# Masking the spread column norms on GpSimd, and scaling and masking in one VectorE operation

## What is computed

```python
# layer 0, per batch; h = relu(layernorm(x)), adj is a 0/1 matrix of 128 x 128
z_l, z_g, v = h @ W_lang.T, h @ W_grav.T, h @ W_V.T
zn  = z_l / max(norm(z_l), 1e-8)
A_l = max(zn @ zn.T, 0) * (1 - eye)                  # language similarities
d2  = max(sq + sq.T - 2 * z_g @ z_g.T, 0)
A_g = exp(-d2 / (2 * sigma**2)) * (1 - eye)
K   = w_l * row_stochastic(A_l * adj) + (1 - w_l) * row_stochastic(A_g * adj)
x   = x + (K @ v) @ W_O.T
# layer 1; h2 = relu(layernorm(x))
x   = x + adj.T-weighted sum of h2 over the nodes + bias
```

## Time and profile before

| what | value |
|---|---|
| time, median of 3 runs | 1271.28 us (1269.57 to 1271.44) |
| the profiled execution, its own time | 1269.61 us |
| its span in the trace | 1267.7 us |
| TensorE busy, share of the span | 1241.2 us, 98% |
| VectorE | 1058.5 us, 83% |
| ScalarE | 694.5 us, 55% |
| GpSimd | 574.7 us, 45% |
| granted TensorE clock, mean | 0.996 |

### The profile page before, as it was taken

One profiled execution on the slowest core, in us unless ns is written; L12 is line 12 of the kernel. 1 busy time (PEld: TensorE's weight loads), 2 busy tenths in 40 slices (PEclk: granted clock), 3 DMA queues, 4 the chain that ended last, 5 costly groups with the idle time before them and its releaser, 6 DMA issues.

```text
span 1267.7 us, 22572 instructions
## 1 busy us (share of the span) xinstructions
PE 1241.2 (98%) x6324; PEld 1039.6 (82%) x6324; DVE 1058.5 (83%) x1826; ACT 694.5 (55%) x1324; POOL 574.7 (45%) x964
## 2 busy tenths in 40 slices
PE   7999999999999999999999999999999999999996
PEld 6878888888888888888888888888888888888884
DVE  5678888988888988888898888898888898888777
ACT  5346555456645456655446655546655545654543
POOL 1115553434554434554434555444555443455433
PEclk9999999999999999999999999999999999999998
DMA  6232424342333343333343232344242444243201
GB/s 243 34 72 81 106 54 95 99 108 81 102 71 78 99 108 87 95 79 70 99 108 97 86 93 56 99 108 103 79 108 49 99 101 108 79 103 69 47 34 66
DMA packets 308894, 112.55 MB, mean 89 GB/s; under 512 B 269840, under 2 KB 269968, under 8 KB 308880
## 3 DMA queue, kind: packets, MB, share of 16 engines
q1 hardware_dynamic: 177360, 95.78, 27.2%
q10 hardware_dynamic: 131520, 16.60, 7.9%
HBM read 46.20 MB, written 33.62 MB: 63 GB/s over the span
## 4 chain that ended last, share of the span: by engine, by line
PE 93%; DVE 4%; ACT 1%; issue 1%; DMA 1%; POOL 0%; SPq 0%; DVEq 0%; ACTq 0%
PE ring L866 75%; PE p_ps L866 15%; PE p_ps L939 2%; PE kt_ps L879 1%; DMA h2f<-in_L_gnn_W_grav 1%; DVE x_out L688 0%; DVE bn L568 0%; DVE y_lo L557 0%; ACT h L379 0%; DVE bn L637 0%; DVE x_ring L631 0%; DVE y_lo L784 0%; DVE deg L602 0%; DVE v_lo L784 0%; DVE hT_lo L557 0%
## 5 line engine op out<-in xcount | busy, mean ns | idle before, releaser
L301 POOL TENSOR_TENSOR x_out<-x_ring,bias_sb 128x512 f32<-128x512 f32 x128 | 162.8, 1295 | 499.9 <-DVE bn L637 499.9
L866 PE MATMUL ring<-hT_hi,Lw_hi 128*128 128x512 f32 x640 | 256.9, 401 | 4.9 <-DVE hT_lo L576 2.1
L406 ACT ACTIVATE y_hi<-ring 128x512 fp32r<-128x512 f32 x256 | 148.3, 592 | 206.5 <-PE ring L866 203.7
L866 PE MATMUL ring<-hT_hi,Lw_lo 128*128 128x512 f32 x640 | 250.6, 392 | 0.0
L866 PE MATMUL ring<-hT_lo,Lw_hi 128*128 128x512 f32 x640 | 250.2, 391 | 0.0
L866 PE MATMUL ring<-MT_hi,hT_hi 128*128 128x512 f32 x512 | 203.0, 396 | 0.0
L557 DVE TENSOR_TENSOR v_lo<-ring,v_hi 128x512 fp32r<-128x512 f32 x128 | 88.5, 692 | 136.8 <-ACT v_hi L442 136.8
L866 PE MATMUL ring<-MT_hi,hT_lo 128*128 128x512 f32 x512 | 200.0, 391 | 0.0
L866 PE MATMUL ring<-MT_lo,hT_hi 128*128 128x512 f32 x512 | 199.9, 390 | 0.0
L308 POOL TENSOR_TENSOR h_lo<-h2f,h_hi 128x512 fp32r<-128x512 f32 x124 | 158.0, 1296 | 84.8 <-ACT h_hi L476 84.8
L557 DVE TENSOR_TENSOR y_lo<-ring,y_hi 128x512 fp32r<-128x512 f32 x256 | 169.2, 680 | 28.4 <-ACT y_hi L406 28.3
(11 more groups left out here) (160 smaller groups left out, 2537.0 us busy)
## 6 DMA issues: line engine op xcount, KB each, us to landing
x_ring<-in_x SPq DMA_DIRECT2D x32, 1024.0 KB, 5.5
out<-x_out SPq DMA_DIRECT2D x128, 256.0 KB, 2.2
h_turned<-h SPq DMA_DIRECT2D x248, 64.0 KB, 2.1
h_turned<-h ACTq DMA_DIRECT2D x248, 64.0 KB, 2.1
rn_cols<-rn_dram SPq DMA_DIRECT2D x31, 256.0 KB, 3.9
x_ring<-in_L_gnn_W_lang SPq DMA_DIRECT2D x4, 256.0 KB, 5.6
h2f<-in_L_gnn_W_grav SPq DMA_DIRECT2D x1, 1024.0 KB, 9.2
chain<-in_L_gnn_W_O SPq DMA_DIRECT2D x1, 1024.0 KB, 13.0
```

What stands on the lines that cost most here:

```text
L301: pool.tensor_tensor(x_out[:, b], x_rows(g, b), bias_sb[:, :], ALU.add).then_inc(x2b_ready, 1)
L406: act.activation(y[0][:, a, :, l], bank(n).rearrange("p (b m) -> p b m", b=GB), ACT.Copy)\
L866: mm = pe.matmul(out, lhsT, rhs, start=(k == 0), stop=(k == len(terms) - 1))
```

## The change

`rn_dram` and `rn_cols` are laid out batch by batch, with the nodes contiguous; the store to DRAM therefore writes single elements. GpSimd multiplies `rn_cols` in place by the mask (`mask_norms`) behind its four `h2_lo`, and waits for the spread there. VectorE's `similarities` is gone; `mask_l` now takes the maximum of A and 0 and multiplies by the masked `rn_cols` in one operation, and waits for `rn_masked`. Only the last group keeps two operations (`mask_l_last`). `a_ready` counts two steps per group instead of three.

```diff
-        rn_cols = sb("rn_cols", [P, P, GB])
+        rn_cols = sb("rn_cols", [P, GB, P])
-        rn_dram = nc.dram_tensor("rn_dram", [P, GB], F32).ap()
+        rn_dram = nc.dram_tensor("rn_dram", [GB, P], F32).ap()
...
             def spread_norms(g):
                 sp.wait_ge(rn_step, RN_STEPS * g + 1)
-                sp.dma_start(rn_dram, rn[:, 0]).then_inc(rn_stored, 16)
+                sp.dma_start(rn_dram.rearrange("b p -> p b"), rn[:, 0], allow_slow_non_contiguous=True).then_inc(rn_stored, 16)
                 sp.wait_ge(rn_stored, 16 * g + 16)
-                sp.dma_start(rn_cols[:, :, :], rn_dram.unsqueeze(0).to_broadcast([P, P, GB])).then_inc(rn_spread, 16)
+                sp.dma_start(rn_cols[:, :, :], rn_dram.unsqueeze(0).to_broadcast([P, GB, P])).then_inc(rn_spread, 16)
...
+            def mask_norms(g):
+                pool.wait_ge(rn_spread, 16 * g + 16)
+                by_col = mask[:, :].unsqueeze(1).to_broadcast([P, GB, P])
+                pool.tensor_tensor(rn_cols[:, :, :], rn_cols[:, :, :], by_col, ALU.mult).then_inc(rn_masked, 1)
...
                     for b in range(GB):
                         h2_lo(i - 1, b)
+                if after:
+                    mask_norms(i)
...
-            def similarities(g, last=False):
-                if last:
-                    dve.wait_ge(r_done, 1)
-                else:
-                    dve.wait_ge(rn_spread, 16 * g + 16)
-                dve.wait_ge(s_ready, g + 1)
-                by_col = r_ps[:, :, :] if last else rn_cols[:, :, :].rearrange("p m b -> p b m")
-                dve.tensor_tensor(A[:, :, 0], A[:, :, 0], by_col, ALU.mult).then_inc(a_ready, 1)
             def mask_l(g):
-                dve.wait_ge(a_ready, 3 * g + 1)
+                dve.wait_ge(rn_masked, g + 1)
+                dve.wait_ge(s_ready, S_STEPS * (g + 1))
+                dve.scalar_tensor_tensor(out=A[:, :, 0], in0=A[:, :, 0], scalar=0.0,
+                                         in1=rn_cols[:, :, :],
+                                         op0=ALU.max, op1=ALU.mult).then_inc(a_ready, 1)
+
+            def mask_l_last(g):
+                dve.wait_ge(r_done, 1)
+                dve.wait_ge(s_ready, S_STEPS * (g + 1))
+                dve.tensor_tensor(A[:, :, 0], A[:, :, 0], r_ps[:, :, :], ALU.mult).then_inc(a_scaled, 1)
+                dve.wait_ge(a_scaled, 1)
                 dve.scalar_tensor_tensor(out=A[:, :, 0], in0=A[:, :, 0], scalar=0.0, in1=maskb,
                                          op0=ALU.max, op1=ALU.mult).then_inc(a_ready, 1)
```

More of the change, by code:

```diff
@@ L30, in gnn_pair @@
     RN_STEPS = 2
+    S_STEPS = 1
     blk = {ac: n for n, ac in enumerate(TRI)}
@@ L171, in gnn_pair @@
         diag_ready = sem("diag_ready")
-        rn_step = sem("rn_step")
+        rn_step, rn_masked, a_scaled = sem("rn_step"), sem("rn_masked"), sem("a_scaled")
         def passes(hi_lo_lhs, hi_lo_rhs):
@@ L600, in row_factors @@
             def row_factors(g):
-                dve.wait_ge(a_ready, 3 * g + 3)
+                dve.wait_ge(a_ready, 2 * g + 2)
                 dve.tensor_reduce(deg[:, 0], A, AX.X, ALU.add).then_inc(deg_step, 1)
@@ L738, in iteration @@
                         output(i - 1, b, n + b)
-                similarities(i)
                 mask_l(i)
@@ L768, in last_chain @@
                 sum_s(i)
-                similarities(i, last=True)
-                mask_l(i)
+                mask_l_last(i)
                 mask_g(i)
```

## The result

The changed kernel took **1412.55 us** (median of 5 runs, 1411.79 to 1414.38) against 1271.28: ratio 1.1121 (95% interval 1.1106 to 1.1137), 141 us slower. The profiled execution took 1411.79 us, with a span of 1410.0.

What follows compares the result with a forecast made beforehand. TensorE was taken as busy nearly throughout, the turn's end hanging on GpSimd's `h_lo` chain from the eighth y block. Gains of 2.0 and 0.3 us, 2.3 in sum, took 1271.28 to 1269.0 us; range 1261.5 to 1275.

Steps and rivals of the forecast that it cites:

- The store: On SP's queue: 512 runs of 4 bytes take 2.5 us until the spread may go, bounds 1.7 and 5.6.
- rival B: Slow store delays GpSimd's `mask_norms`; TensorE pays one for one beyond a 5.2 us store; 1282 at 5.6; chance 0.12.
- 0.73 us free behind 640.3: From 640.3 on, delaying GpSimd's `mask_norms` costs nothing up to today's `KT_lo`, 0.73 us; beyond that one for one.
- `hT_lo` at about 1 us: On VectorE at the turn's end: `hT_lo` is stretched to about 1 us by GpSimd's `h_lo`.
- GpSimd's operation: `mask_norms`, 128x512, behind the last `h_lo`: taken at 1.28 us, bounds 1.28 and 2.0.
- Rival A: Turn's end hangs on ScalarE's copies, so the whole K·v wait is gained: 9.2 us plus 0.3, 1261.8; chance 0.12.
- the K·v wait: First weight load of the K·v products waits for `kt_split`: 0.33 us of TensorE per turn, to go in 28 turns.
- Rival C: `mask_norms` starts before `hT_lo`, so the first `x_out` comes 1.28 us later: 36 us, 1307; chance 0.05.
- Rival D: Nothing arrives: merged operation dearer (1.07), or small operations excluded long enough to use up the lead: 1271.3; chance 0.16.
- The sum of 2.3 us: Total gain: 28 x 0.07 = 2.0 us, plus 0.3 at the fifth y block's weight load waiting for `y_lo`.
- the third residual addition: On VectorE, it waits for the third K·v product; an earlier K·v gains 0.07 us per turn, 2.0 in 28.
- The place of the new wait: `mask_norms` waits for the spread on GpSimd, before `norm1`; norms usable from about 640.3, spread lands at 638.3, hidden.

Runs made afterwards that it cites:

- the first experiment: Changed kernel with the old store and norms layout (128 runs of 16 bytes, node by node), L592 reading the norms strided: 1265.38 us, ratio 0.9963.
- the fifth: Kernel of the first experiment, with the statistics of the group's last two residual additions ahead of all of the next group's: 1257.55 us, ratio 0.9896.
- the second experiment: Kernel before with only the new store and layout; L586 and L592 stay apart, nothing goes to GpSimd: 1338.52 us, ratio 1.0536.

## Why the prediction was wrong

**The step that failed is "The store".** The prediction bounded the new store by 1.7 us (the old store) and 5.6 (the `scal` loads at the start) and took 2.5, from the row of `h` with as many runs. It took 8.7, in the kernel and by itself. Both neighbours were chosen by the number and size of runs; what counted was how the runs lie against each other in DRAM. The turns of `h` have 512 runs each, and 512 runs that lie apart take only 2.7 us, near what I took; 512 side by side take 8.7. The upper bound was no better: a load says nothing about neighbouring writes, and no row of before showed 4-byte writes side by side. With no neighbour of the same kind the top of the range should have stood open, and with it rival B's share, which I held at 0.12 because the slack of 1.9 us looked ample.
The rule of the Trainium skill cited there (DMA: Bandwidth & Descriptors, Rules for kernel authors), that a strided last dimension becomes one descriptor per element and should be rearranged, pointed the right way. Descriptors alone do not explain the price: 2.7 us against 8.7 for the same 512 elements.

**Rival B was the mechanism, with two terms off.** It said one for one, and the turns show 1.52 against 1.55. It let the cost begin at a store of 5.2 us, with 0.73 us free behind 640.3, which is 0.72 us before the turn's start. Extended to a turn of 37.61, the changed kernel's line has the cost begin 0.75 us before the turn's start, so of the 0.73 nothing is left, and the point is a store of about 9.15 − 0.75 − 3.9 = 4.5 us. The later turn shown above gives the reason. From the end of L307 to `normalize` it takes 681.63 − (675.99 + 1.26) = 4.38 us; the prediction had 607.5 + 37.74 − 641.6 = 3.64, and the 0.74 between them is as much as the margin. `norm1`'s small operations now run while VectorE works through L592 and `y_lo`, and two of them take 0.68 and 0.67 us, where such an operation alone takes 0.20. The prediction had allowed 0 to 0.6 us for that and not set it against the margin. And the spread lands after 4.8 us, not 3.9. Worked by its own line, (8.7 − 5.2 + 0.9) x 28 = 123 us; with the point at 4.5, (8.7 − 4.5 + 0.9) x 28 = 143; measured 141, or 147 over the kernel with the old store.

**What held.** With the store left as it was, the rest came as foreseen: `hT_lo` at about 1 us (0.99), the first weight load 0.6 us behind `x_out` (0.55), a turn of 37.66 (37.65 in the one shown, 37.61 on average), `normalize` 0.89 us later where 0.65 was worked out, and L592 at 0.69 us where it reads contiguously (1.08 with the stride). GpSimd's operation was taken at 1.28: it took 1.27 in the changed kernel, but 1.54 here, where it starts beside `hT_lo`. Rival A falls: the K·v wait is gone in the first experiment and its time did not come, until the fifth moved the chain too. Rival C does not occur: `hT_lo` starts before L307 (637.35 against 637.76). Rival D does not hold for these parts: their gain, 4.9 us with an interval of 2.9 to 6.4, excludes nought.

**A smaller term was mis-sized.** The sum of 2.3 us lies just under that interval. The mean turn is 0.14 us shorter, of which 0.07 was counted for the third residual addition. The traces of before and of the first experiment show where it arises (start in the turn, mean of the 24 middle turns): the `y_lo` of the eighth y block moves from 15.11 to 15.06 us, the third addition from 16.98 to 16.87, the last `h_lo` from 35.25 to 35.12. So the third addition gave its 0.07, and the y blocks gave 0.04 per turn, 1.3 us in 30 turns where the sum has 0.3. The weight loads' waits for `y_lo` fell by the 2.0 us that the prediction set out (3.6 to 1.6); running matmuls covered less of it than I took.

**The place of the new wait** was treated as free because the norms seemed early. It was right to name what is queued behind it, `norm1`; but moving the wait from VectorE to GpSimd brought its due time forward by 2.4 us (from 1.66 us into the turn to −0.75), and by the second experiment that is about half of the loss.

## What to carry to other kernels

When an edit changes how a small transfer lies in DRAM, look at which runs become neighbours, not only at their count and size; where no row shows writes of that kind, leave the upper bound open, and put no wait that depends on it in front of work that others need. Before valuing a stall, follow the end of the turn back to its own chain: here the K·v wait was worth 0.07 us a turn alone and 0.3 once the chain beside it had moved, so two edits together gave 12.8 us where their single gains add up to 7.5. The version to keep is the fifth experiment's kernel: the merged operation with the old store, and the residual's statistics first.

## What the runs showed of the hardware that was not expected

Stores of small runs to DRAM are slow when the runs begin close to each other: 128 runs of 4 bytes take 7.07 us at 4 bytes from start to start, 2.61 at 8, and 1.40 at 16, 32 or 64. Runs of 8 bytes side by side (8 from start to start) behave like the 4-byte runs at that distance (3.11). In all forms of 128 runs neighbouring runs come from different partitions. In the 512 runs 8 bytes apart, four neighbours at a time come from one partition, and the price of the nearness is about the same: 4.31 against 2.7 for 512 runs 64 bytes apart, where 128 runs take 2.61 against 1.40 (rounds between 3.3 and 4.7, and 2.6 and 4.0). Whether runs of one partition would be as slow 4 bytes apart, and whether it matters which transfer engine writes them, was not tried, so the mechanism behind it stays open.
